# A two-layer transformer kernel: layer 1 in a new order, layer 0's memsets first, four rotated halves and the first batch rotated at once

## What is computed

```python
# layer 0: 16 heads of 16, rotary positions, causal
q, k, v = heads(x @ Wq.T), heads(x @ Wk.T), heads(x @ Wv.T)
q = q * cos + rotate_every_two(q) * sin          # k alike
attn = softmax(q @ k.T / 4 + causal_mask)
x = layernorm(x + merge(attn @ v) @ Wo.T)
x = layernorm(x + chosen_expert(x) * its_score)  # 8 experts, one for each token
# layer 1: window of 128 keys, and a gated path over 64 pooled positions
local = window_attention(qkv(x)); remote = latent_attention(x, pooled(x)) @ rout_w
g = sigmoid(local @ gl_w + remote @ gr_w)
x = layernorm(x + (g * local + (1 - g) * remote) @ out_w + out_b)
x = layernorm(x + chosen_expert(ln(x)) * its_gate)  # one expert for each batch
```

## Time and profile before

| what | value |
|---|---|
| median of 3 runs | 1327.37 us (1327.31 to 1329.86) |
| the profiled execution, its own time | 1328.57 us |
| its span in the trace | 1326.8 us |
| mean granted clock of TensorE | 0.956 |
| layer 0's attention, from the start | until about 560 us |
| layer 1, from its first stretch | from about 716 us to the end |
| PE busy in 0 to 58 us | 24.16 of 58 us |
| PE busy in 321 to 387 us (layer 0) | 63.61 of 66 us |
| PE busy in 600 to 716 us (experts) | 115.40 of 116 us |
| PE busy in 902.4 to 967.8 us (layer 1) | 59.82 of 65.4 us |

### The profile page before, as it was taken

One profiled execution on the slowest core, in us unless ns is written; L12 is line 12 of the kernel. 1 busy time (PEld: TensorE's weight loads), 2 busy tenths in 40 slices (PEclk: granted clock), 3 DMA queues, 4 the chain that ended last, 5 costly groups with the idle time before them and its releaser, 6 DMA issues. The chain is left out here.

```text
span 1326.8 us, 32573 instructions
## 1 busy us (share of the span) xinstructions
PE 1163.5 (88%) x12513; PEld 762.4 (57%) x12513; DVE 927.4 (70%) x2335; ACT 605.6 (46%) x1144; POOL 276.5 (21%) x294
## 2 busy tenths in 40 slices
PE   5399799999999998699998789898989898989875
PEld 3145466565655664399995355556565656555542
DVE  4798487877888783367777577777777677777643
ACT  1046255555556565155552135454546354635431
POOL 3201121212212011111113221032323232303113
PEclk8699899999999999799999989999999999999888
DMA  5443534435152435252211633505151515140000
GB/s 185 111 123 96 142 90 105 133 89 153 57 136 70 109 102 192 75 196 73 72 50 48 175 89 103 122 26 153 35 144 42 138 35 145 42 109 19 3 17 16
DMA packets 68264, 126.81 MB, mean 96 GB/s; under 512 B 8320, under 2 KB 58128, under 8 KB 64784
## 3 DMA queue, kind: packets, MB, share of 16 engines
q1 hardware_dynamic: 65040, 116.33, 31.7%
q0 software_dynamic: 3072, 8.41, 2.0%
HBM read 83.27 MB, written 40.66 MB: 93 GB/s over the span
## 5 line engine op out<-in xcount | busy, mean ns | idle before, releaser
L589 ACT ACTIVATE arena<-pair 128x512 f32<-128x512 f32 x320 | 185.2, 597 | 140.0 <-PE pair L463 134.6
L1531 ACT ACTIVATE second_probs<-pair 128x512 f32<-128x512 f32 (+1 forms) x256 | 135.6, 541 | 200.2 <-PE pair L1393 162.2
L669 DVE TENSOR_REDUCE first_maxima<-bank 128x1 f32<-128x512 f32 (+3 forms) x235 | 145.2, 634 | 20.8 <-PE bank L434 20.0
L1691 DVE TENSOR_REDUCE second_maxima<-bank 128x3 f32<-128x480 f32 (+1 forms) x160 | 105.2, 660 | 61.0 <-PE bank L1360 58.9
L456 PE MATMUL pair<-stacks 128*128 128x512 bf16 (+3 forms) x512 | 122.5, 301 | 19.9 <-DMA stacks<-first_m_turned 13.3
L431 PE MATMUL bank<-stacks 96*128 96x512 bf16 (+3 forms) x343 | 88.1, 310 | 22.2 <-DVE first_maxima L669 16.0
L1385 PE MATMUL pair<-second_q_stack,second_k_stack 128*32 128x160 bf16 (+4 forms) x2048 | 84.0, 231 | 4.0 <-ACT second_probs L1531 2.8
L669 DVE TENSOR_REDUCE first_maxima<-pair 128x1 f32<-128x512 f32 (+3 forms) x117 | 74.4, 636 | 18.3 <-PE pair L434 17.8
L463 PE MATMUL pair<-constants_bf 128*128 128x256 bf16 (+1 forms) x320 | 80.5, 251 | 0.0
L895 PEld LDWEIGHTS pair<-expert_xsT,expert_W_near 128*128 128x128 f32 x624 | 77.1, 195 | 4.7 <-ACT expert_xsT L938 2.9
L895 PE MATMUL pair<-expert_xsT,expert_W_near 128*128 128x128 f32 x624 | 78.1, 279 | 1.6 <-ACT expert_xsT L938 1.6
(11 more groups left out here) (344 smaller groups left out, 2565.4 us busy)
## 6 DMA issues: line engine op xcount, KB each, us to landing
stacks<-parked SPq DMA_DIRECT2D x96, 256.0 KB, 5.2
parked<-first_parts SPq DMA_DIRECT2D x32, 384.0 KB, 2.8
second_q_stack<-parked SPq DMA_DIRECT2D x48, 256.0 KB, 5.3
second_k_stack<-parked SPq DMA_DIRECT2D x48, 256.0 KB, 8.3
parked<-second_parts SPq DMA_DIRECT2D x30, 384.0 KB, 2.5
expert_xs<-sorted_x SPq DMA_DIRECT2D x39, 128.5 KB, 2.1
sorted_y<-expert_ys SPq DMA_DIRECT2D x39, 128.0 KB, 1.7
first_xT<-in_xT SPq DMA_DIRECT2D x8, 512.0 KB, 4.2
```

The costliest lines, as they stand in the source:

```text
L589: act.activation(PT[:, s:s + len(heads), lo:lo + each], ex[n % 2][:, 0:len(heads) * each].rearrange("p (h q) -> p h q", h=len(heads)), ACT ...
L669: dve.tensor_reduce(nm[:, i, qt, heads[0]:heads[0] + len(heads)], mx[n % 3][:, 0:wide].rearrange("p (h k) -> p h k", h=len(heads)), AX.X, ...
L1531: act.activation(PT[:, s:s + len(heads), lo:lo + each], scores[:, :, 0:each], ACT.Exp, scale=SCALE).then_inc(lp["exps"], 1)
L1691: dve.tensor_reduce(nm[:, i, :, :].rearrange("p t h -> p (t h)")[:, first:end], mx[n % 2][:, 0:(end - first) * wide].rearrange("p (u k) -> ...
```

## The change

Four things are changed, none of them in what is computed.

1. **Layer 0, memsets.** The item `ones` of batch 0 moves from -3.1 to -9.9, which makes it DVE's first. DVE's wait for the rotation tables (`rope_in`) moves from the top of its list to the first `rope`.
2. **Layer 0, rotated halves.** `halves` holds four blocks, not two. A `rope` waits for the `lo` of four blocks before. In batch 0 all eight `rope` items stand ahead of the first `rest`.
3. **Layer 0, weights.** The one DMA of Wq, Wk and Wv (768 KB) becomes two: Wq first (256 KB) ahead of x (512 KB); Wk and Wv (512 KB) behind x. PE waits for the second at `qk` of block 2.
4. **Layer 1, order.** `MOVED` has new numbers and `AHEAD1` is added, so the items of layer 1 stand in another order. All `max` items are 0.397 unit earlier; the order of POOL is the same.

The diff, without what only repeats, and with a few lines of the new `MOVED`:

```diff
@@ front0(): time written out for layer 0's first batch
-            time["qk", 0, 2 * p + n, 0] = t + 0.1 * n - 0.15 * p
+            time["qk", 0, 2 * p + n, 0] = (-8, -7.65)[p] + (0.1, 0.005)[p] * n
             for j in range(2):
-                time["rope", 0, 2 * p + n, j] = t + 0.2 + 0.1 * n + 0.04 * (j if n == 0 else 1 - j)
+                time["rope", 0, 2 * p + n, j] = (-7.8, -7.64)[p] + (0.1, 0.02)[p] * n + (0.04, 0.01)[p] * (j if n == 0 else 1 - j)
@@ schedule0()
-                       (-0.55, "fold"), (-0.5, "fold_in"), (-3.1, "ones")):
+                       (-0.55, "fold"), (-0.5, "fold_in"), (-9.9, "ones")):
@@ layer0_attention()
-        halves, parts = sb("halves", [P, 2, 2, S]), sb("parts", [P, 2, 3, S], bf16)
+        halves, parts = sb("halves", [P, 4, 2, S]), sb("parts", [P, 2, 3, S], bf16)
...
-                sp.dma_start(w["qkv0"][:, :, :], a["qkv0"].rearrange("(c p) n -> p c n", p=P)).then_inc(lp["w_in"], 16)
+                per_chunk = a["qkv0"].rearrange("(c p) n -> p c n", p=P)
+                sp.dma_start(w["qkv0"][:, :, 0:D], per_chunk[:, :, 0:D]).then_inc(lp["w_in"], 16)
...
                         if b == 1:
+                            sp.dma_start(w["qkv0"][:, :, D:3 * D], per_chunk[:, :, D:3 * D]).then_inc(lp["wkv_in"], 16)
                             sp.dma_start(w["rope"][:, :, :], a["rope"]).then_inc(lp["rope_in"], 16)
...
                     if kind == "qk":
+                        if b == 0 and i == 2:
+                            pe.wait_ge(lp["wkv_in"], 16)
...
                 dve.memset(m["half"][:, :], -0.5).then_inc(lp["half_set"], 1)
-                dve.wait_ge(lp["rope_in"], 16)
...
                         of = i ^ j
+                        if k == 0 and j == 0:
+                            dve.wait_ge(lp["rope_in"], 16)
                         dve.wait_ge(lp["qk_ps"], 4 * b + of + 1)
-                        if k >= 2:
-                            dve.wait_ge(lp["lo"], k - 1)
+                        if k >= 4:
+                            dve.wait_ge(lp["lo"], k - 3)
                         bank, before = work["qk", b, of, 0]
-                        dve.tensor_tensor(halves[:, k % 2, j, :], wk[bank][:, :], w["rope"][:, j, :], ALU.mult)\
+                        dve.tensor_tensor(halves[:, k % 4, j, :], wk[bank][:, :], w["rope"][:, j, :], ALU.mult)\
...
@@ layer 1: new table of single items, applied at the end of front1()
+AHEAD1 = {
+    ("hi", 0, 2, 0): -0.102, ("qk", 1, 2, 0): -0.294, ("rest", 0, 0, 0): 0.328, ("rest", 0, 1, 0): -0.029,
+    ("rest", 1, 3, 0): -0.048, ("v", 0, 0, 0): -0.292,
+}
...
+    for item, late in AHEAD1.items():
+        time[item] += late
@@ MOVED, a few of its entries
-    "bd": {None: -0.092}, "choose": {None: -0.007}, "g_exp": {None: 0.08}, "gather": {None: -0.036}, "h_in": {None: -0.033},
+    "bd": {None: -1.463}, "choose": {None: -0.114}, "fin": {0: -0.088}, "g_exp": {None: 0.08}, "gather": {None: -0.036},
...
+    "lt_in": {0: 0.031, 1: 0.146}, "max": {None: -0.397}, "mix": {1: -0.049}, "near": {None: 0.003}, "new": {None: -0.049},
...
+    "out": {0: 0.066}, "park": {1: -0.138}, "qk": {0: -0.048, 1: -0.047, 2: -0.609, 3: -0.048},
+    "r": {0: -0.19, 1: 0.073, 2: 0.073, 3: 0.073}, "r_in": {0: 0.017, 1: 0.017, 2: 0.11, 3: 0.108},
...
+    "rvr": {0: -0.037}, "rvr_in": {1: 0.09}, "send": {None: 0.272}, "stack": {0: 0.164, 1: 0.941}, "turn_a": {0: 0.082, 1: 0.023},
```

28 lines of the change are left out of this document (13 added, 15 removed).

## The result

The changed kernel takes 1320.2 us in the median of 20 executions (1312.26 to 1326.26), the kernel before 1327.07 (20 executions). The ratio is 0.9944 (0.9932 to 0.9957): faster by 7 us, where 19 to 20 were forecast. It is the value of the first rival, 1320.

The account below looks back on a forecast made before the run. PE, busy for 88% of the span, was taken as the bound, with one long wait in layer 0 and short ones in layer 1. Layer 0's -7 and layer 1's -13 sum to -20: 1308 us, range 1299 to 1323.

Parts of the forecast that it names:

- Layer 1's -13: Layer 1's new order: -2.2 us a batch, between bounds of -4.0 and 0, over six batches.
- That is 4.0 of 5.5 us: Layer 1: the new order could remove 4.0 of the 5.5 us of short PE waits in a batch.
- I take all 0.7: Layer 1: both `l_sum` ahead of `lo` fill DVE's 1.58 us idle and remove PE's 0.7 us wait for `norm`.
- rival 3: Layer 1: the K stack comes too late for the earlier `max`, and the kernel is slower; 1331 us, chance 0.05.
- `v`, 0.5: Layer 1: an `exp` between `values` and `v` covers 0.5 of PE's 0.6 us wait.
- `lt_in`, 0.5: Layer 1: `g_sum` about 1.3 us sooner, but an `exp` ahead of `lt_in`; 0.5 of the 0.9 us `qk` wait goes.
- The first `max` of a batch can meet the K stack: Layer 1: a counter-effect of the earlier `max`, which might wait for the K stack's DMAs; 1 to 4 us left.
- rival 1: Layer 1's waits only change their names, at `r` before `lt_in` or the second `out` before `add`; 1320 us, chance 0.20.
- Layer 0's -7.1: Layer 0: -8.65 for the memsets and 1.5 for the later chain; ends -9.4 and -4.2 us.
- -8.65: Layer 0: DVE's memsets, with the idle ahead of them, leave the place where PE waits for DVE; 8.65 us.
- +1.5: Layer 0: all eight `rope` first make the second `lo` 2.0 us later; 1.5 us reaches the first maximum.
- In the new order no `sum` runs then: Layer 0: without `sum` on POOL, first `rest` to second `lo`'s end takes 4.1 us, not 4.5.

Follow-up runs that it names:

- e2: Kernel before with only layer 1's new order: 1328.58 us, ratio 1.0001 to the kernel before.
- f1: Changed kernel with the second `l_sum` of a layer 1 batch back behind `lo`: 1318.51 us, ratio 0.9945 to the kernel before.
- h1: Changed kernel with ACT's `g_exp` of layer 1 moved behind `lt_in`: 1317.28 us, ratio 0.9947 to the kernel before.
- e1: Changed kernel with layer 1 in its old order, so layer 0's part alone: 1321.29 us, ratio 0.9953 to the kernel before.
- f2: Changed kernel with layer 1's `l_p` ahead of the fourth `mid` and `lo` behind the first two `norm`: 1322.6 us, ratio 0.9979 to the kernel before.
- e3: Kernel before with only layer 0's memsets moved first and the `rope_in` wait behind them: 1319.51 us, ratio 0.9936 to the kernel before.
- e4: Kernel before with four buffers of halves, split weights and rotated first batch, memsets at their old time: 1330.56 us, ratio 1.0025.

## Why the prediction was wrong, step by step

**Layer 1's -13 failed.** The step is "That is 4.0 of 5.5 us", and from it "I take -2.2, a little over half" and "Six batches give -13". Measured: 0.7 us in a steady batch of the changed kernel, -0.4 in e2's first, and a ratio of 1.0001 for the whole of it, at most 2.7 us by its interval. By item:
- `l_sum`, "I take all 0.7": nothing (f1). I counted the idle time that it fills, and not that it frees `l_p` to run beside `lo`. I had applied the Trainium skill's rule on the shared port pair in layer 0, where it favoured the change, and not here, where it speaks against it: `g_sum` comes 0.25 us sooner behind the store (16.78 against 17.03) and not 1.3. The same 1.58 us of idle stand in the prediction twice: here as filled by `l_sum`, and in rival 3 as slack that absorbs a late `lo`.
- `v`, 0.5: the wait for `v_in` went, and one of the same 0.6 us for `rests` came. The gather's wait fell by 0.4 us (0.7 to 0.3), where 0.1 was counted.
- `lt_in`, 0.5: it grew from 0.9 to 1.2. It hung on the same 1.3 us, and its place behind `g_exp` stayed. h1 shows that even without this wait nothing is gained.
- `turn_a` 0.9, `up` 0.7, `turn_z` and the rest 0.6: these waits went, from 2.6 to 0.6 us together. PE then came sooner to the waits that were left, and four of the seven (2.2 of 3.9 us) end with DVE.
- PE's idle time fell by 1.5 us (5.58 to 4.09 in the windows), its busy time rose by 0.78. The twelve matmuls of `qk` that hold a single bank account for 0.4 (5.6 to 6.0 us); the rest I can't place.
- "The first `max` of a batch can meet the K stack": it did, 6.2 us in five batches. I had it as a rival with 1 to 4 us of slack and with nothing in the sum. The signs of being wrong named it too.
- "At the start of layer 1 more `max` are done", counted at 0 with the end: in the traces 1.9 us more at the start, and 5.9 us less in the batch before last, by the clock and by work done earlier. Neither was in the sum.

So rival 1 was what happened, in its value and its heading, that waits only change their names. The two places that it named, `r` ahead of `lt_in` and the second `out` ahead of `add`, aren't in PE's list, and that the median is its 1320 to 0.2 us is luck, since layer 0 gave 5.6 us in e1 and not 7. Its "against", that seven waits would each have to be replaced, was wrong: in h1 one unbroken stretch of DVE work took over the wait that was removed, and in f2 the K stack did.

**Layer 0's -7.1 was right in sign and near in size.** e1 gave -5.6 in time, and the eleven traces with this front -3.7 to -5.95 at the first maximum, -4.9 in the mean. The term of the memsets, -8.65, measured -7.4 to -7.8 (e3). The term of the rotated batch, "+1.5" with up to 0.7 given back at the front, measured +2.8 at the first maximum in the mean of all traces and +3.9 in e4: mis-sized by a factor of about two. "In the new order no `sum` runs then": none runs beside the first `rest`, which is 0.68 us as the Trainium skill's rule on the shared port pair gives it, but one runs beside the second `lo`, which costs 1.05. From the first `rest` to the end of that `lo` it took 5.2 us, where 4.1 were counted.

The range of 1299 to 1323 held the time.

## What to carry to other kernels

When a step is moved into an engine's idle time, ask what it releases, and on which engine that then runs: here the released GpSimd instruction slowed the Vector instruction beside it by as much as the idle time had been. A list of short waits isn't a sum to be collected: find the engine that works without a gap across several of them, ask what shortens that stretch, and then look what is next (here the K stack). Edits that each come up against the next bound can show nothing alone, and are worth trying together before they are given up.

## What the runs showed of the hardware

A VectorE tensor_tensor with two SBUF inputs (128x512, 0.69 us alone) took 2.22 us when a GpSimd tensor_tensor of 1.90 us started 0.25 us ahead of it: that is nearly what was left of the other (1.65 us) and its own 0.69, so the loss is the rest of the GpSimd instruction, and not a share of it. In h1 it started 0.34 us behind and took 2.12 us (1.56 left of the other). Beside a `sum` it took 1.74 us.

The batch before last took 59.74 us at a granted clock of 0.89 before, and 53.81 us at 0.97 in the changed kernel, with 44 matmuls fewer in it. Before the fall TensorE had worked for 0.93 of 3 us, and the clock then stayed at the lower level (0.50) while it was busy for the next 3 us. The median execution of the changed kernel is 8 us above its fastest, and the granted clock goes with it (0.968 in the fastest, 0.958 in the slowest), so one trace is not a measurement of 0.5%.
